# Four-layer network on one core: the gathered experts of the second layer reordered and their table built by short operations, the two norms of the third layer put in one phase

## The reference, cut to what matters

```python
for each layer:
    xn = layernorm(x)
    s = mixer(xn)
    g = silu(experts(xn))
    x = x + s * g
```

```python
scores = (x_flat @ Wg.T).T
top_vals, token_idx = top_k(scores, 512)
token_w = softmax(top_vals, axis=-1)
xg = x_flat[token_idx]
h = silu(einsum('eic,ehc->eih', xg, W1)) * einsum('eic,ehc->eih', xg, W3)
y = einsum('eih,ech->eic', h, W2) * token_w[..., None]
out = zeros_like(x_flat).at[token_idx.reshape(-1)].add(y.reshape(-1, c))
```

```python
norm = layer_norm(feat, ln_g, ln_b)
scores = norm @ centroids.T
```

## Time and profile before

| | before |
|---|---|
| median of 3 runs | 2463.93 us (2463.89 to 2464.37) |
| profiled execution, its own time | 2479.12 us |
| its span, first to last instruction | 2477.3 us |
| instructions | 43017 |
| busy: PE, DVE, ACT, POOL | 2052.9, 1398.5, 1050.1, 630.8 us |
| granted TensorE clock, mean over the span | 0.868 of full speed |

### The profile page before, as it was taken

One profiled execution on the slowest core, in us unless ns is written; L12 is line 12 of the kernel. 1 busy time (PEld: TensorE's weight loads), 2 busy tenths in 40 slices (PEclk: granted clock), 3 DMA queues, 4 the chain that ended last, 5 costly groups with the idle time before them and its releaser, 6 DMA issues. The chain is left out here.

```text
span 2477.3 us, 43017 instructions
## 1 busy us (share of the span) xinstructions
PE 2052.9 (83%) x16486; PEld 1373.4 (55%) x16486; DVE 1398.5 (56%) x3332; ACT 1050.1 (42%) x2493; POOL 630.8 (25%) x692
## 2 busy tenths in 40 slices
PE   5989999977689997975527686644999999999798
PEld 2556666656556764543315354433666666666465
DVE  2027777634544444556358993023676767677577
ACT  3236656522335443210045432223666666666322
POOL 3017900011200001006751003124333333333100
PEclk9989999978679998986756565775899999999999
DMA  2062020021000001201260002121000000000000
GB/s 61 18 38 11 4 34 2 2 58 20 36 16 1 1 1 53 67 1 25 35 182 14 19 19 62 56 70 44 1 1 1 1 1 1 1 1 1 1 18 18
DMA packets 110330, 61.68 MB, mean 25 GB/s; under 512 B 65288, under 2 KB 104752, under 8 KB 108976
## 3 DMA queue, kind: packets, MB, share of 16 engines
q1 hardware_dynamic: 101728, 50.14, 8.9%
q0 software_dynamic: 7680, 8.40, 1.8%
q10 hardware_dynamic: 720, 0.40, 0.1%
HBM read 37.41 MB, written 21.50 MB: 24 GB/s over the span
## 5 line engine op out<-in xcount | busy, mean ns | idle before, releaser
L2767 ACT ACTIVATE l_prob<-l_ps,l_neg_max 128x128 f32<-128x128 f32 (+1 forms) x512 | 208.2, 419 | 45.1 <-DVE l_neg_max L2827 40.1
L1471 ACT ACTIVATE l0a_prob<-l0a_pst 128x1024 f32<-128x1024 f32 x128 | 131.0, 1024 | 119.9 <-PE l0a_pst L1389 119.9
L2652 POOL TENSOR_TENSOR l_prob<-l_prob,l_total 128x256 f32<-128x256 f32 x128 | 78.4, 612 | 373.2 <-DVE l_total L2835 373.2
L1522 DVE TENSOR_REDUCE l0a_peak<-l0a_ps 128x4 f32<-128x1024 f32 x128 | 156.2, 1221 | 16.0 <-PE l0a_ps L1384 13.9
L2823 DVE TENSOR_TENSOR l_ps<-l_ps,future 128x512 f32<-128x512 f32 x128 | 89.3, 698 | 109.0 <-PE l_ps L2698 109.0
L1384 PE MATMUL l0a_ps<-l0a_k,l0a_q 32*128 32x256 f32 x1024 | 146.5, 406 | 3.0 <-ACT l0a_prob L1471 2.5
L474 ACT ACTIVATE l0e_hidden<-l0e_ph,l0f_b 128x512 f32<-128x512 f32 x128 | 87.9, 687 | 141.5 <-PE l0e_ph L389 141.5
L1389 PE MATMUL l0a_pst<-l0a_q,l0a_k 32*128 32x256 f32 x1024 | 145.8, 400 | 0.2 <-ACT l0a_prob L1471 0.2
L399 PEld LDWEIGHTS l0e_py<-l0f_w,l0e_hidden 128*128 128x128 f32 x1024 | 119.6, 192 | 36.0 <-ACT l0e_hidden L474 32.0
L389 PE MATMUL l0e_ph<-l0f_h_ch,l0f_w 128*128 128x512 f32 x256 | 125.4, 604 | 11.9 <-PEq L43 11.9
L2653 POOL TENSOR_TENSOR l_prob<-l_prob,l_total 128x512 f32<-128x512 f32 x128 | 133.0, 1039 | 0.0
(11 more groups left out here) (487 smaller groups left out, 4877.7 us busy)
## 6 DMA issues: line engine op xcount, KB each, us to landing
l_band<-zero SPq DMA_DIRECT2D x16, 272.0 KB, 3.9
x_tok<-in_x_dram SPq DMA_DIRECT2D x2, 2048.0 KB, 8.2
l2f_w<-in_L_ffn_w_dram SPq DMA_DIRECT2D x2, 2048.0 KB, 9.8
l_rows<-l_band SPq DMA_DIRECT2D x16, 256.0 KB
l1f_w<-in_L_ffn_W_dram SPq DMA_DIRECT2D x3, 1024.0 KB, 7.0
gd_tri<-gp_tri SPq DMA_DIRECT2D x8, 256.0 KB, 2.0
l0f_w<-gd_tri SPq DMA_DIRECT2D x8, 256.0 KB, 13.2
gd_tri<-l0f_w SPq DMA_DIRECT2D x8, 256.0 KB, 9.2
```

The costliest lines, as they stand in the source:

```text
L1471: act.activation(prob[:, (n // 2) % 2, pair, :, :].rearrange("p g t s -> p g (t s)"), pst[:, :, :, :].rearrange("p g t s -> p g (t s)"), A ...
L1522: dve.tensor_reduce(to, ps[m % 2][:, :, :, :], AX.X, ALU.max, negate=True).then_inc(max_ready, 1)
L2767: act.activation(prob[:, m % 4, h, cols], ps[m % 2][:, h, cols], ACT.Exp, bias=neg_max[:, m % 4, h, t:t + 1], accum_out=total[:, m % 4, h, ...
```

## The change

In layer 1's experts: `place` is built by 32 tensor-scalar operations of 128 columns instead of one tensor-tensor operation of 4096; `what` by two operations instead of five. DVE runs `find(0)` right behind `build(0)`, and both gates of an expert in front of `find` and the next `build`. TensorE lists tokens behind `up(e, 1)` instead of ahead of `up(e, 0)`. The save of the turned rows and the weighing move from DVE to ACT. In layer 2: one phase instead of two. The second norm has no statistics of its own: with r the first deviation's inverse, the normalized block has mean 0 and variance r*r*var, and POOL works out the second from it. DVE multiplies by it and by the gain in one operation a block and adds the shift; TensorE turns both results and makes logits in the same phase. The band's stores of zeros go to SP's queue in layer 1's mixer phase, and the fetch of layer 2's expert weights to the new phase.

```diff
+def norm_and_norm(nc, c, st, norm_tok, gain, shift, cent, score, fetch, fetched, ready, ffn, ffn_fetched, landed):
...
+            @block.sync
+            def _(sp):
+                for to, what in fetch:
+                    sp.dma_start(to, what).then_inc(fetched, 16)
+                for to, what in ffn:
+                    sp.dma_start(to, what).then_inc(ffn_fetched, 16)
...
+                def statistics(g):
+                    dve.wait_ge(gate_ready, g + 1)
+                    link(combine_group(dve, st, gate[:, g % 3, :, :], rows(g), link))
+                    for j in range(GB):
+                        ins = dve.bn_stats(stats[:, g, j, :], st.x[:, g * GB + j, :])
+                    link(ins)
+                    for j in range(GB):
+                        ins = dve.bn_aggr(mv[:, g, j, :], stats[:, g, j, :])
+                    ins.then_inc(stats_ready, 1)
+
+                def centre(g):
+                    dve.wait_ge(first_ready, g + 1)
+                    dve.scalar_tensor_tensor(bias[:, g, :], mv[:, g, :, 0], -1.0, first[:, g, :], ALU.mult, ALU.mult).then_inc(bias_ready, 1)
+
+                def scale(g):
+                    y = norm_tok[:, rows(g), :]
+                    dve.wait_ge(norm_ready, g + 1)
+                    dve.wait_ge(second_ready, g + 1)
+                    for j in range(GB):
+                        ins = dve.scalar_tensor_tensor(y[:, j, :], st.xn[:, g * GB + j, :], second[:, g, j:j + 1], gain, ALU.mult, ALU.mult)
+                    link(ins)
+                    dve.tensor_tensor(y, y, shift.unsqueeze(1).to_broadcast([P, GB, D]), ALU.add).then_inc(again_ready, 1)
+
+                for m in range(GRP + 2):
+                    if m < GRP:
+                        statistics(m)
+                    if 0 <= m - 1 < GRP:
+                        centre(m - 1)
+                    if m == 2:
+                        dve.wait_ge(*ready)
+                    if 0 <= m - 2 < GRP:
+                        scale(m - 2)
+                dve.wait_ge(routed, GRP)
+                dve.tensor_copy(score[:, :, :], logits[:, :, :].rearrange("p b e -> p e b"))
...
+                for g in range(GRP):
+                    r, t, var = first[:, g, :], second[:, g, :], mv[:, g, :, 1]
+                    pool.wait_ge(stats_ready, g + 1)
+                    link(pool.tensor_scalar(r, var, LN_EPS, None, ALU.add))
+                    link(pool.tensor_tensor(r, r, c.minus_half[:, :], ALU.pow))
+                    pool.tensor_tensor(t, r, r, ALU.mult).then_inc(first_ready, 1)
+                    pool.wait_ge(first_ready, g + 1)
+                    link(pool.tensor_tensor(t, t, var, ALU.mult))
+                    link(pool.tensor_scalar(t, t, LN_EPS, None, ALU.add))
+                    pool.tensor_tensor(t, t, c.minus_half[:, :], ALU.pow).then_inc(second_ready, 1)
...
 def layer1_mix_and_choose(...)
...
-                sp.wait_ge(kept_in_dram, 32)
+                for b in range(BATCH):
+                    rows = band[b * SEQ * PITCH:(b + 1) * SEQ * PITCH].rearrange("(t p n) -> p t n", t=2, p=P)
+                    sp.dma_start(rows, c.zero[:, :, :]).then_inc(kept_in_dram, 16)
+                sp.wait_ge(kept_in_dram, 16 * (2 + BATCH))
...
 def gathered_experts(...)      # TensorE
...
                 for e in range(E + 1):
                     if e < E:
                         turn(e)
-                    if e + 2 < E:
-                        list_tokens(e + 2)
-                    if e < E:
                         up(e, 0)
                     if e >= 1:
                         down(e - 1)
                     if e < E:
                         up(e, 1)
+                    if e + 2 < E:
+                        list_tokens(e + 2)
...
+                def save_xt(e):
+                    act.wait_ge(turned, e + 1)
...
+                    act.activation(xt[:, e % 2, :], pt[:, :, :].rearrange("p b t -> p (b t)"), ACT.Copy).then_inc(xt_saved, 1)
...
+                def weigh(e):
+                    act.wait_ge(y_ready, e + 1)
...
+                    for j in range(GB):
+                        ins = act.activation(y[:, e % 2, j, :], py[:, j, :], ACT.Copy, scale=weight[:, e, j:j + 1])
+                    ins.then_inc(y_saved, 1)
+
+                for e in range(E + 1):
+                    if e < E:
+                        save_xt(e)
+                        open_gate(chunks * e)
+                    if e >= 1:
+                        weigh(e - 1)
+                    if e < E:
+                        open_gate(chunks * e + 1)
...
-                    for v in range(V):
-                        value = r.number[:, :, v] if v < 2 else r.piece[:, e, :, v - 2]
-                        dve.tensor_tensor(what[:, e % 2, :, :, v], mark[:, e % 2, :, :], value.unsqueeze(2).to_broadcast(wide), ALU.mult)
-                    full = [P, BLK, P]
-                    dve.tensor_tensor(place[:, e % 2, :, :], r.lane[:, e, :].unsqueeze(2).to_broadcast(full),
-                                      r.column[:, :].unsqueeze(1).to_broadcast(full), ALU.is_equal).then_inc(built, 1)
+                    for first, values in ((0, r.number[:, :, :]), (2, r.piece[:, e, :, :])):
+                        n = values.shape[-1]
+                        dve.tensor_tensor(what[:, e % 2, :, :, first:first + n], mark[:, e % 2, :, :].unsqueeze(3).to_broadcast([P, BLK, GB, n]),
+                                          values.unsqueeze(2).to_broadcast([P, BLK, GB, n]), ALU.mult)
+                    for b in range(BLK):
+                        ins = dve.tensor_scalar(place[:, e % 2, b, :], r.column[:, :], r.lane[:, e, b:b + 1], None, ALU.is_equal)
+                    ins.then_inc(built, 1)
...
                 build(0)
+                find(0)
                 build(1)
-                find(0)
                 find(1)
                 build(2)
-                for e in range(E + 1):
-                    if e < E:
-                        save_xt(e)
+                for e in range(E):
+                    gate(chunks * e)
+                    gate(chunks * e + 1)
                     if e + 2 < E:
                         find(e + 2)
-                    if e < E:
-                        gate(chunks * e)
-                    if e >= 1:
-                        weigh(e - 1)
                     if e + 3 < E:
                         build(e + 3)
-                    if e < E:
-                        gate(chunks * e + 1)
```

More of the change, by code:

```diff
@@ L1161, in pairs, with layers01 @@
         return found
-def layers01(nc, c, st, a, landed):
+def layers01(nc, c, st, a, landed, band):
     E, F = 8, 256
@@ L1562, in _, with layer1_mix_and_choose @@
                             add_out(n)
-def layer1_mix_and_choose(nc, c, st, w, ready, fetch, fetched, spent, score, chosen, r, sent, made):
+def layer1_mix_and_choose(nc, c, st, w, ready, fetch, fetched, spent, score, chosen, r, sent, made, band):
     INNER, STATES, TAPS = 256, 16, 4
@@ L2543, in layers23 @@
                      (m_w2[:, :], a["L2_attn_w2"]), (m_w1[:, :], a["L2_attn_w1"]), (v[:, :], a["L2_attn_v"])]
-            for b in range(BATCH):
-                rows = band[b * SEQ * PITCH:(b + 1) * SEQ * PITCH].rearrange("(t p n) -> p t n", t=2, p=P)
-                fetch.append((rows, c.zero[:, :, :]))
             bias = a["L2_ffn_b2"]
```

122 lines of the change are left out of this document (100 added, 22 removed).

## The result

The changed kernel takes 2425.48 us (median of 4 runs, 2423.35 to 2427.0), the kernel before 2463.91 beside it (2460.3 to 2464.37): a ratio of 0.985 with an interval of 0.983 to 0.986, 38.4 us or 1.5% less. Forecast were 29.3 less, 2434.6. The profiled execution is the run of 2423.35 us, with a span of 2421.6.

What follows compares the result with a forecast made beforehand. No engine was near full: POOL's descriptor issue led the experts after DVE's first builds, DVE the norms. Profiled 2479.12 - 18.4 (experts) - 10.9 (norms) = 2449.8 us, or 2434.6 as a median; range 2424 to 2456.

Steps and rivals of the forecast that it cites:

- the likeliest case: Whole kernel: the forecast of 2434.6 us as summed, own range 2427 to 2442, chance 0.52.
- (5): Two norms in one phase: DVE leads at 4.5 us a group, phase 46.4 against 57.3 us, -10.9.
- (1): Experts' `place` on DVE: 32 operations 0.195 us apart take 6.2 us, plus 1.7 on each build.
- (2): Experts' `what` on DVE: two operations take 2.0 us a build against 2.19 for five, saving 0.2.
- (3): Experts' new order on DVE and TensorE, weighing on ACT: first scatter 8.7 us earlier.
- (4): Experts from first scatter on: four long POOL instructions go, -13.7 us; port sharing adds 3, slower weighing at the end 1.0.
- The +3: Experts: POOL's descriptor instructions lengthened beside the 32 `place` operations, 3 us in all; bounds nothing to 25.
- (6): DMAs: moved band stores and earlier expert weights cost 0; ACT's two copies of 0.6 us sit in its idle time.
- POOL shut out: Experts: POOL gets the port only midway or at the end of the 32 operations; 2444 or 2457 to 2462; chance 0.17.
- DVE waits: Experts: `place` operations wait for POOL's descriptor work, DVE's cycle passes 12.4 us; priced 2475; chance 0.11.
- One column a cycle: Experts: `place` operations 0.26 us apart, build 10.1 us, first scatter 6.3 later; 2441 to 2444; chance 0.10.
- POOL leading the norms: Norm phase: POOL sets the period at 6.0 us a group, no gain there; 2444 to 2447; chance 0.08.

Runs made afterwards that it cites:

- experiment 4: The changed kernel with `what` put back to five operations of 128 columns instead of two: 2427.75 us, ratio 0.986 to the kernel before.

## Why the prediction was right

The direction and the mechanism held, and the time is 9 us below the forecast, inside the range but outside the 2427 to 2442 given to the likeliest case. Most of the miss lies in the experts, and its large parts have one sign; the norms came right in part by luck, see (5). The two traces give -25.9 us for the experts (forecast -18.4) and -11.4 for the norms (-10.9).

**(1) place in 32 operations.** 0.198 us each, 6.35 against 6.2. Right. Beside POOL a build's `place` takes 6.4 to 6.85.

**(2) what in 2 operations: mis-sized.** From 2.19 to 2.0 us, it said; measured from its first operation to `place` are 0.84 (1102.94 - 1102.10), and by experiment 4 1.68 for the five. (The 2.19 adds the lengths of operations that overlap.) The saving is 0.84 a build, not 0.2. The step that failed is "I take 2.0, since the stride of the output and the type stay". The estimate from the Trainium skill's rule on adjacent pairs (Vector Engine (DVE) Microarchitecture Reference, section 5.2) was 0.9 to 1.3; the trace lies a little below it. The page has measured the rule on 32-bit words only, so for 16-bit elements it was a guess that came out in the right direction.

**(3) The order.** From the first `mark` to the first scatter 46.0 us became 34.3: -11.8, forecast -8.7. The third `place` ends 25.9 us after the first `mark` (forecast 27.2), 1.3 less, mostly by (2). From there to the first scatter stand 8.35 us, not 9.1 + 1.0: 1.7 less. Of these 0.5 are ACT's weighing, 1.14 us from PSUM where the row taken, 1.65, reads SBUF. The other 1.2 stand with TensorE between the end of that `place` and the weighing: 6.1 us at a granted clock of 1.00, after up products beside the build since 1121.31, where the kernel before had 7.3 us at 0.60, after 5.13 us of idle. Neither the list's new place nor the first `find`'s has a run of its own.

**(4) POOL from there on.** From the first to the last scatter 102.8 us became 88.4: -14.4, forecast -9.7. The four long instructions went. The +3 for what comes in place of them is mis-sized: the stretch is 1.5 us above its undisturbed 69.4, where it was 1.4 besides the long ones before, so almost nothing came. The slower weighing (+1.0) doesn't show; the wait for the seventh result is 2.41, and was 3.21.

**(5) The norms.** Period 4.47 (4.5), phase 45.7 (46.4), and by itself -10.3 in the medians (-10.9). The mechanism, DVE's period, is right. That the phase is so near is in part luck: POOL's chain took 1.22 and 0.22 us where 1.5 and 2.5 stood, and the end behind the last shift add took 7.1 where 5.6 stood.

**(6) Cost 0 for the stores and for "ACT's two copies sit in its idle time".** The 16 band stores take 19.72 us of issue in the mixer phase (12.37 in the norms before), and the first `mark` doesn't come later for it (1101.77, before 1103.46). The copies' 0 is true as a cost, but the reasoning around it was not: I split the gain into -8.7 for the order and -13.7 for the short operations as if each stood alone. Put next to each other, E is 158.0 before, 156.0 with short operations only, 151.7 with all but the short `place`, 165.0 with all but ACT's share, and 132.2 with everything. The step that fails is the independence of the two terms, and the runs show that they are worth 26 us only together. The prediction had DVE's cycle at 10.9 us, under POOL's 12.4; that sum of busy times holds only because the copy is on ACT, so that TensorE's products run beside a build. With the copy on DVE the cycle is 16.8.

**The rivals.** POOL shut out: not with this form, but 32 two-input operations of the same length do just that (E 156.9), so here the case turned on the kind of operation. DVE waits: one `place` operation in the trace lasts 0.59 us instead of 0.27, but a whole build never more than 0.5 us over its 6.35. One column a cycle at 0.26 apart, and POOL leading the norms, did not come.

## What to carry to other kernels

A copy and a weighing of 0.7 us each can be worth thirty when they stand behind a long piece of table work on an in-order engine: add up the cycle from the waits, not from the busy times. Where GpSimd issues descriptors beside VectorE, look at the form as well as at the length of VectorE's operations: 32 one-input operations freed it, while an instruction caught in a row of 32 two-input ones of the same length was held to the end of the row, which takes 6.5 us where the single long one takes 4.4. When several edits are made on one stage, try each with and without the others: here the short operations alone won 2 us, everything but the short `place` 6, and all together 26.
